# Second attention of a transformer layer: the order of score fills, maxima fills and value products on TensorE

## The reference

```python
Q = (hs @ q_w + q_b).reshape(B, S, H, HD).transpose(0, 2, 1, 3)
K = (hs @ k_w + k_b).reshape(B, S, H, KPH).transpose(0, 2, 1, 3)
V = (hs @ v_w + v_b).reshape(B, S, H, KPH).transpose(0, 2, 1, 3)
scores = jnp.einsum('bhsk,bhtk->bhst', Q[..., :KPH], K) / math.sqrt(KPH)
attn = jax.nn.softmax(scores, axis=-1)
ao = jnp.einsum('bhst,bhtv->bhsv', attn, V)
```

## Time and profile before

| | us |
|---|---|
| median of 3 runs | 1904.3 (1903.35 to 1906.33) |
| the profiled execution, its time | 1917.99 |
| its span, first to last instruction | 1916.3 |
| the 16 groups of the second attention | about 768 of the span |

### The profile page before, as it was taken

How to read it: one execution, slowest core, us unless ns; L and a number is a source line. 1 busy time by engine, 2 the same in 40 slices (tenths; PEclk the granted TensorE clock), 3 DMA queues, 4 the chain that set the end, 5 groups by cost and what they waited for, 6 DMA issues and landing times. The chain is left out here.

```text
span 1916.3 us, 40640 instructions
## 1 busy us (share of the span) xinstructions
PE 1651.5 (86%) x14982; PEld 732.3 (38%) x14982; DVE 1397.3 (73%) x2330; ACT 1273.9 (66%) x1224; POOL 392.5 (20%) x532
## 2 busy tenths in 40 slices
PE   1499999999999999963788898888888988889995
PEld 1244444444444444431222232223322232266774
DVE  5067777888888888886677777776777677547888
ACT  4276666666666666633777777776777678855776
POOL 4011212333333333322022002200120111120004
PEclk8599999999999999975899999997998799989998
DMA  4411000000000000005011001100110010000001
GB/s 116 91 49 38 35 34 35 35 34 34 34 35 35 34 34 34 3 2 117 1 42 43 18 29 43 43 18 30 42 43 17 18 40 18 2 14 9 15 11 44
DMA packets 54106, 65.64 MB, mean 34 GB/s; under 512 B 11189, under 2 KB 36309, under 8 KB 53975
## 3 DMA queue, kind: packets, MB, share of 16 engines
q1 hardware_dynamic: 51328, 59.00, 10.5%
q10 hardware_dynamic: 2646, 4.90, 1.3%
HBM read 19.30 MB, written 14.68 MB: 18 GB/s over the span
## 5 line engine op out<-in xcount | busy, mean ns | idle before, releaser
L1298 ACT ACTIVATE arena<-psum 128x1024 f32<-128x1024 f32 x512 | 517.2, 1028 | 180.5 <-PE psum L1120 171.2
L1497 DVE TENSOR_REDUCE arena<-psum 128x2 f32<-128x1024 f32 x336 | 406.1, 1221 | 97.8 <-PE psum L1147 95.5
L642 ACT ACTIVATE arena<-psum 128x2048 f32<-128x2048 f32 (+1 forms) x160 | 273.5, 1709 | 232.5 <-PE psum L527 229.8
L1135 PE MATMUL psum<-arena 128*32 128x256 f32 x4096 | 345.4, 418 | 1.4
L697 POOL TENSOR_SCALAR_AFFINE_SELECT arena<-arena 128x512 f32<-128x512 f32 (+1 forms) x160 | 169.5, 1076 | 592.3 <-ACT arena L642 592.3
L544 PE MATMUL psum<-arena,hs 128*64 128x512 f32 (+3 forms) x1536 | 283.0, 496 | 2.7 <-POOL arena L697 2.2
L1120 PE MATMUL psum<-arena 32*128 32x512 bf16 x1024 | 207.4, 403 | 88.8 <-DVE arena L1497 52.7
L1147 PE MATMUL psum<-arena 32*128 32x512 bf16 x1024 | 209.9, 411 | 35.9 <-DMA arena<-latent_kpm 13.2
L527 PE MATMUL psum<-arena 64*128 64x512 f16 (+3 forms) x2304 | 216.3, 325 | 4.9 <-DVE arena L732 3.6
L732 DVE TENSOR_TENSOR arena<-arena 128x1024 f16<-128x1024 f32 x64 | 78.4, 1225 | 180.0 <-ACT arena L621 180.0
L1504 DVE CUSTOM_DVE_ANT_0 arena<-psum,arena 128x512 f32<-128x512 f32 x176 | 114.6, 689 | 109.9 <-PE psum L1147 94.5
(11 more groups left out here) (211 smaller groups left out, 2268.4 us busy)
## 6 DMA issues: line engine op xcount, KB each, us to landing
arena<-arena SPq DMA_DIRECT2D x32, 512.0 KB, 3.0
arena<-arena SPq DMA_DIRECT2D x48, 128.0 KB, 2.3
arena<-latent_q SPq DMA_DIRECT2D x64, 64.0 KB, 2.0
arena<-latent_k SPq DMA_DIRECT2D x64, 64.0 KB, 2.0
arena<-latent_kpm SPq DMA_DIRECT2D x64, 64.0 KB, 2.0
arena<-arena SPq DMA_DIRECT2D x32, 96.0 KB, 2.6
X<-in_L_attn_states SPq DMA_DIRECT2D x4, 512.0 KB, 12.7
arena<-arena SPq DMA_DIRECT2D x32, 64.0 KB, 1.8
```

Source lines behind the costliest of these rows:

```text
L642: nc.scalar.activation(probs[g], SC[:, :, 0:WIDTH[g]], ACT.Exp, scale=DH ** -0.5).then_inc(exp_done, 1)
L1135: last = nc.tensor.matmul(OT[ROWS * c:ROWS * (c + 1), h * HALF // 2:(h + 1) * HALF // 2], v_cols[par][:, kt, 2 * pr + i, :], e_probs[u % 4 ...
L1298: nc.scalar.activation(e_probs[u % 4], src, ACT.Exp, scale=KD ** -0.5).then_inc(e_done, 1)
L1497: nc.vector.tensor_reduce(half_tops[:, kh, qt, 2 * pr:2 * pr + 2], src.rearrange("p (i c) -> p i c", i=2), AX.X, ALU.max).then_inc(top_don ...
```

## The change

The order of TensorE's program inside a group is changed, and nothing else. The maxima of item u + 24 come straight after the scores of item u, with their waits; the side work follows. Value products are no longer done at every item: at odd u those of items u - 3 and u - 2 are done together, behind that item's fills and side work, and at even u none. The table `HELD` goes, since items 3 and 19 do the same two products by the new rule.

```diff
--- before.py
+++ after.py
@@ -939,7 +939,6 @@
 
         TOPS1_AT, TOPS0_AT = 11, 27
         TURN1_AT, INVERT1_AT, SCALED1_AT, TURN0_AT, SCALED0_AT = 2, 4, 12, 18, 24
-        HELD = {TURN1_AT: (), TURN1_AT + 1: (0, 1), TURN0_AT: (), TURN0_AT + 1: (16, 17)}
         PROJECT_AT, LAST_PROJECT_AT = (14, 20), 26
         HS_AT, QK_AT, LV_AT = (0, 3), (6, 9), 14
 
@@ -1235,23 +1234,23 @@
                             g, m = divmod(LEAD + u - 2, ITEMS)
                             item_read(pe, n + g, m)
                         scores(par, u, slot(gi, u, 0))
-                        if u >= 2:
-                            for v in HELD.get(u, (u - 2,)):
-                                values(n, par, v)
-                        elif at_least(n, 1):
-                            values(n - 1, 1 - par, ITEMS + u - 2)
+                        g, m = divmod(LEAD + u, ITEMS)
+                        if not (last and g):
+                            rows_here(n + g, m, (par + g) % 2, GROUPS // 2 * b + (gi + g) // 2 + 1)
+                            if gi == GROUPS - 1 and u == SHIFT_AT:
+                                pe.wait_ge(e_done, ITEMS * n + u + 1)
+                            else:
+                                upto(pe, e_done, ITEMS * n + u)
+                            if gi == GROUPS - 1 and u == SHIFT_AT + 1:
+                                item_read(pe, n + g, m - 2)
+                            maxima(n + g, (par + g) % 2, m, slot(gi, u, 1))
                         spare(b, gi, u, last)
-                        g, m = divmod(LEAD + u, ITEMS)
-                        if last and g:
-                            continue
-                        rows_here(n + g, m, (par + g) % 2, GROUPS // 2 * b + (gi + g) // 2 + 1)
-                        if gi == GROUPS - 1 and u == SHIFT_AT:
-                            pe.wait_ge(e_done, ITEMS * n + u + 1)
-                        else:
-                            upto(pe, e_done, ITEMS * n + u)
-                        if gi == GROUPS - 1 and u == SHIFT_AT + 1:
-                            item_read(pe, n + g, m - 2)
-                        maxima(n + g, (par + g) % 2, m, slot(gi, u, 1))
+                        if u % 2 == 1:
+                            for v in (u - 3, u - 2):
+                                if v >= 0:
+                                    values(n, par, v)
+                                elif at_least(n, 1):
+                                    values(n - 1, 1 - par, ITEMS + v)
 
                 pe.wait_ge(hs_ready, 1)
                 for h in range(2):
```

## The result

The changed kernel takes 1980.0 us (median of 4 runs, 1972.3 to 2000.3) against 1905.3 for the kernel before on the same chips: a ratio of 1.040, 95% interval 1.0315 to 1.0485, so it is 4% slower. The profiled execution took 1976.7 us with a span of 1975.0, against 1918.0 and 1916.3; its mean clock over the whole span is 0.910 against 0.931.

What follows compares the result with a forecast made beforehand. Prediction: TensorE, ScalarE and VectorE hand slots round, and waiting for them sets the pace. +16 us at full clock and +17 us from the clock make +33 us, forecast 1937 us, range 1902 to 1985.

Steps and rivals of the forecast that it cites:

- the second case: Second attention: the clock swings between its levels, 300 us at half clock, +76 us, 1980 us; chance 0.16.
- The ring: Ordinary pair of items: score fill, exponential, waiting maxima fill, two value products; 2.82 us, where the reductions' ring took 2.60.
- The step that no row showed: In a pair, from the waiting maxima fill to the value products: taken as 0.31 us, bounds 0.23 and 0.57.
- Two signs: In a pair, reductions end 0.3 and 1.9 us after the first score fill; score fills' waits for VectorE nearly vanish.
- Difference items: Five places a group where ScalarE does three jobs: delays hidden, cost nothing; 24 us if ScalarE were 0.3 us later.
- Side work: Transposes, projection steps and next-batch preparation on TensorE: transposes cost 0.66 us a group; projection and preparation give time back.
- The projection: Projection steps of 1.1 us on TensorE, partly falling into the wait for the exponential: 3 us back.
- The preparation: Preparation of the next batch, taken to behave like the projection: 1 us back.
- The sum at full clock: Second attention: a group goes from 44.6 to 45.8 us; with the small terms, +16 us in all.
- The clock: Second attention: 165 us at half clock, 52 us lost where about 35 were lost before, so +17 us.
- The case that held places were the cause: Held places brought the clock down and it now stays up: faster, 1885 us; chance 0.07.
- The case of the array's own time: TensorE's own time bounds; fewer changes between fills and value products save 56 us: 1848 us; chance 0.04.

Runs made afterwards that it cites:

- y4: Changed kernel with each exponential as two ScalarE instructions of 512 elements a row; 1990.0 us in one run.
- x1: Changed kernel with one value product at every item instead of two at odd items, fills still together; 1882.8 us, ratio 0.9905.
- x4: Changed kernel with one of the two value products moved ahead of the second maxima fill; 1943.5 us, ratio 1.0239.
- y1: Kernel before with the score fills of items 2 and 18 (held places) issued three times into the same slot; 1904.9 us, ratio 0.9989.
- v1: The mirrored order: changed kernel with the two value products at even items instead of odd ones; 1925.9 us, ratio 1.0083.
- x2: Kernel before with value products in pairs at odd items, still between score fill and maxima fill; 1999.6 us, ratio 1.0503.
- x3: Changed kernel with the score fill of each odd item issued twice, as useless work; 1956.7 us, ratio 1.0309.
- y3: Changed kernel with score fills of odd items and maxima fills of even items issued twice; 1935.5 us, ratio 1.0182.

## Why the prediction was right, and where it was not

The measured 1980 us lies in the range, near its upper end, and the sign was right. The forecast of 1937 was 43 us short, 33 us of slowdown where 75 were measured. 1980 is the number of the second case, and that is in part luck: the case had 300 us at half clock in the stage, where the profile has 200, and a smaller loss at full clock.

- **The ring.** 2.82 us was worked out, 2.83 measured. The step that no row showed, from the maxima fill to the values, is 0.32, where 0.31 was taken. The price of the exponential in the ring is shown by y4, that of value products behind the wait by x1 and x4. Two signs were off without harm: the first reduction ends 0.6 after the first score fill and not 0.3, so the second score fill still waits 0.25 for it, and the score fills' waits for VectorE are 70 us and not nearly nothing. That wait lies ahead of the one for the exponential.
- **Difference items** at nothing: the pair in the second timeline above takes 2.83 us, and so does every pair without transposes in that group. Right. The same walk is what I left out for x4.
- **Side work.** The transposes cost 0.33 each (items 10 and 26 begin pairs of 3.16 us). The projection was put at 3 us back and brings about 1: at full clock such a group takes 51.6 us (group 12), 5.6 over a plain one, and 5.9 over it in the order of before (50.5 in y1, group 4). The preparation was put at 1 us back and is a loss: the second groups take 50.6 us at full clock, 4.7 over a plain one, where the kernel before took 48.0, 3.4 over. That is 1.2 a group, about 4 us over three, so the term was of the wrong sign and 5 us off. The walk left out that ScalarE copies in between and hands on the delay: in group 5 a copy of 0.59 stands ahead of the exponential for which the maxima fill of item 6 waits, and this fill goes 1.00 after its score fill.
- **The sum at full clock**, +16. The mirrored order, with the same ring and about the clock of the kernel before, gives +18 to +25, and the groups of the changed kernel at full clock about +23 (15 x 1.35, +4, -1). Right in its mechanism, somewhat small.
- **The clock**, +17. This is the step that failed in size. I took 165 us at half clock in the stage, 73 more than before, and it was 200 in the profiled execution. The base was off too: the profiled execution of the kernel before was one of its slower, at 0.931, and the median one has 0.941. Between the medians, 0.941 and 0.907, the half-clock time of an execution is 225 and about 366 us, 141 us more. At 0.29 us each, and 0.37 by a line through the changed kernel's own four runs, that is 41 to 52 us where I had 17. "A milder place in every pair" was thought of as more falls; what came were three long stretches (70, 55 and 65 us of them in the stage). The price of a us at half clock, 0.315, was about right; the time at half clock was not. Why this order keeps the clock down so long stays open, as v1 shows.
- **The case that held places were the cause** (1885 us) falls with y1. **The case of the array's own time** (1848 us) needed the wait for the exponential to be covered; TensorE stands idle 0.48 us for it in the pair above. x2 has the fewer changes too and is slower still.
- The Trainium skill, "TensorE: Matmul & The Clock Gate", section "A second HAM failure mode: psum-queue depth-cycling", describes what the second case was made of, short idle times that make the clock swing. x3 and y3 agree with it: with those idle times filled, half clock falls from 200 us to 78 and 22. It does not tell v1 from the changed kernel: with the same waits half clock was 41 us of the stage of v1. Nor did the clock of the changed kernel swing more often, with 6 stretches for 15.

## What to carry to other kernels

On an engine that works in order, look at what stands between the producer of a slot and the next fill that waits for its reader, and at what is queued behind that wait. Work that needs nothing new belongs ahead of the wait or spread evenly, not in a block behind it. Look at the clock of every new order, since its idle time does not tell it: four orders with 6.5 to 18.2 us of idle time in a plain group had clocks from 0.907 to 0.946, and not in that order. Compare changes of some per cent at equal clock: each execution's mean clock tells how much of a difference is the ring and how much the clock.

## What the runs showed of the hardware

- Useless matmuls in idle time made a kernel 44 us faster (y3), raising the clock of the stage from 0.88 to 0.99.
- The same ring with its idle time at the other parity, and more of it (v1), kept a mean clock of 0.946, where the changed kernel had 0.907.
- Executions of one and the same kernel differ in clock, 0.928 to 0.951 for the kernel before, and with it in time (1894 to 1922 us). A comparison of single executions of these kernels says little under 1%.
- Value products in the array cost 0.43 us for one that another follows, and 0.57 for one that a fill follows; in a ring limited by waits the difference can't be collected.
